# Three shared feed-forward batches in fp32r parts on one Trainium2 core

## The chip, the cores and the metric

One NeuronCore of one Trainium2 chip runs the whole program. The metric is the device time of one execution in microseconds (us), shown as the median of several runs. The profile is one more execution, taken by the hardware profiler, with times from the start of its span. The engines are called as in the profile: PE (TensorE), DVE (VectorE), ACT (ScalarE), POOL (GpSimd) and SP, which only issues transfers here.

## The reference

The kernel computes one transformer layer on `x` (4 batches of 512 rows, 256 wide) and a context of which only the first 512 rows of each batch are seen through the causal mask:

```
x = x + attention(layernorm(x), context)          # 16 heads of 16
h = layernorm(x)                                  # 2048 rows of 256
logits = h @ gate_w.T                             # 8 experts
the two best experts of each row, weights by softmax
out = sum over the two: weight * (silu(h @ wg.T) * (h @ wu.T)) @ w_down.T     # 384 hidden columns
shared = silu(h @ sg_gate.T) * (h @ sg_up.T) @ sg_down.T                      # 384 hidden columns, every row
x = x + shared + out
```

The change lies in the line `shared`, and in the preparation of the expert weights.

## The kernel before

All is float32 in value. A product of two float32 operands runs in one of two ways here. Either both operands are given to PE as float32; or each is split into a high part (an fp32r copy) and a low part (the rest, also fp32r), and PE sums three fp32r products, high x high, high x low and low x high. The experts use the second way, the shared batches the first.

The engines run five programs side by side, ordered by hand, which wait for one another on counted semaphores. After attention the order is this. PE turns the normalised rows `xn2` of a batch into columns `xn2T` (L751), makes the router's logits (L760), and between these the shared feed-forward of a batch `b`: `shared_up` (L854) makes blocks `n = 3b + m`; a block is gate and up for 128 hidden columns and the 512 rows of the batch. ACT takes the silu of the gate half (`shared_silu`, L1145), DVE multiplies it by the up half (`shared_h`, L1397) into `sg`, and `shared_down` (L865) multiplies by `w_sd`; DVE adds the result to the rows (`shared_y`, L1419). Two pairs of PSUM banks hold blocks in turn. Batches 0 to 2 run in this stage, batch 3 at the end of the kernel behind the experts (L999).

DVE's routing runs beside it: the two best experts (L1426 to L1440), the weights, for which ACT makes one exponential (L1158), the ranks by products with triangles of ones (L891), and the slot of each row in lists of 128-row tiles; the lists come from one-hot rows (`hot_slots`, L1492) by 32 products (L906). POOL then gathers rows of a tile by an indirect transfer from the DRAM copy `normed_rows` (`rows_in_tile`, L583). That copy is stored by SP for batches 0 to 2 (L447) and by ACT for batch 3 (L1151).

The expert weights `wup` (two transfers of 3 MB, L454) go out on SP's queue when attention has released its memory. ACT makes the eight high pieces `wup_hi` (`hi_parts`, L1159; 1536 columns each) and DVE the eight low pieces `wup_lo` (`lo_part`, L1498); the first expert product (L933) waits for all eight. From there 39 tiles follow in a loop of fixed order (L975): transposes, three-part products up and down, and an indirect transfer that adds the result rows (L587).

The rows `xn2`, the columns `xn2T` and `sg` lie in one region `moe` (L199). Stores of `xn2` to DRAM must have landed before that part of the region is written again.

## Time and profile before

| | |
|---|---|
| median of 3 runs | 495.11 us (494.94 to 496.69) |
| the profiled execution's own time | 494.46 us |
| its span, first to last instruction | 492.4 us |
| mean granted TensorE clock | 0.995 of full speed |
| busy: PE, DVE, ACT, POOL | 93%, 63%, 43%, 40% of the span |

Matmuls are pipelined, so their durations overlap; the step from one start to the next is what one costs. A float32 product shows as two records. In a row of a timeline stand the start, the duration, the engine, the line, the operation, output and inputs, and the idle time before it with what ended it; "x4" means that four instructions in a row are merged into one.

### The profile page before, as it was taken

The page shows a single profiled execution, that of the slowest core. Times are in us where ns is not written, and L with a number is a line of the kernel's source. Part 1 is how long each engine was busy: PE and PEld are TensorE (multiplying, and loading weights), DVE is VectorE, ACT ScalarE, POOL GpSimd, SP SyncE. Part 2 cuts the span into 40 slices and gives each one's busy share as a digit, 9 for nine tenths or more (in the row PEclk, how much of TensorE's full clock was granted, in tenths as well). Part 3 has the DMA queues.
Part 4 walks back from the last instruction along what each step waited for, and adds up shares of the span by engine and source line. Part 5 has one row for each costly group of instructions (what it writes and reads, how often), then busy time and mean ns, then how long its engine had stood idle before and what let it go on. Part 6 is the DMA issues. An engine that isn't in the chain of part 4 may idle for free.

```text
span 492.4 us, 10465 instructions
## 1 busy us (share of the span) xinstructions
PE 457.4 (93%) x3237; PEld 322.0 (65%) x3238; DVE 312.2 (63%) x651; ACT 211.8 (43%) x421; POOL 196.0 (40%) x204
## 2 busy tenths in 40 slices
PE   7979999999999999999978999999999999999992
PEld 6754444654447444564555546699999999999852
DVE  4985757477563856647975895955455555554446
ACT  2255666527572566656764253332332223223210
POOL 4113544214541337302622003036676666665420
PEclk9999999999999999999999999999999999999997
DMA  8593422422124021310398901014444444444389
GB/s 272 101 230 101 126 72 72 140 69 72 63 76 150 32 97 38 115 64 2 98 379 322 327 2 43 0 39 72 76 64 65 74 75 64 65 72 68 36 208 333
DMA packets 45575, 53.86 MB, mean 109 GB/s; under 512 B 7760, under 2 KB 41872, under 8 KB 44912
## 3 DMA queue, kind: packets, MB, share of 16 engines
q1 hardware_dynamic: 34320, 39.77, 25.2%
q0 software_dynamic: 7488, 10.31, 13.3%
q10 hardware_dynamic: 3744, 3.47, 2.7%
q8 instruction: 14, 0.23, 0.2%
q14 instruction: 9, 0.07, 0.1%
HBM read 27.09 MB, written 13.67 MB: 83 GB/s over the span
## 4 chain that ended last, share of the span: by engine, by line
PE 68%; DVE 15%; ACT 6%; issue 5%; DMA 4%; SPq 1%; POOL 0%; DVEq 0%; ACTq 0%; POOLq 0%
PE set_a L628 7%; PE set_b L658 6%; PE set_a L679 6%; PE set_a L934 6%; PE set_a L933 6%; PE set_a L935 6%; PE set_b L648 4%; DVE attention L1317 3%; ACT attention L1084 3%; PE set_b L952 3%; PE set_a L670 3%; PE set_a L842 3%; PE set_b L953 3%; PE set_b L954 3%; PE set_b L943 2%
## 5 line engine op out<-in xcount | busy, mean ns | idle before, releaser
L1317 DVE TENSOR_REDUCE attention<-set_a 128x2 f32<-128x1024 f32 (+2 forms) x96 | 95.9, 1040 | 25.1 <-PE set_a L630 23.0
L1084 ACT ACTIVATE attention<-set_b 128x512 f32<-128x512 f32 (+1 forms) x176 | 87.8, 570 | 50.2 <-PE set_b L648 36.6
L532 POOL TENSOR_SCALAR_AFFINE_SELECT attention<-attention 128x512 f32<-128x512 f32 x64 | 42.6, 679 | 100.5 <-ACT attention L1084 100.5
L592 POOL DMA_INDIRECT sum_rows<-moe,token_of x39 | 61.8, 1585 | 43.9 <-issue 29.8
L648 PE MATMUL set_b<-attention 99*128 99x512 bf16 (+3 forms) x256 | 59.2, 303 | 7.1 <-ACT attention L1084 5.7
L628 PE MATMUL set_a<-attention 96*128 96x512 bf16 (+3 forms) x256 | 60.5, 302 | 4.9 <-DVE attention L1317 4.7
L1184 ACT ACTIVATE moe<-set_a 128x384 f32<-128x384 f32 x39 | 19.1, 490 | 105.2 <-PE set_a L935 95.6
L584 POOL DMA_INDIRECT e_x<-normed_rows,token_of x39 | 39.4, 1011 | 61.3 <-DVE token_of L1516 34.9
L1541 DVE TENSOR_TENSOR moe<-set_a,moe 128x384 f32<-128x384 f32 x39 | 21.7, 557 | 63.0 <-issue 36.3
L628 PEld LDWEIGHTS set_a<-attention 96*128 96x128 bf16 x256 | 24.9, 97 | 44.3 <-DVE attention L1317 17.2
L933 PE MATMUL set_a<-wup_hi,e_xT_hi 128*128 x156 | 53.0, 340 | 0.0
L934 PE MATMUL set_a<-wup_lo,e_xT_hi 128*128 x156 | 52.8, 339 | 0.0
L935 PE MATMUL set_a<-wup_hi,e_xT_lo 128*128 x156 | 52.8, 338 | 0.0
L630 PE MATMUL set_a<-maskb,identb 128*128 128x128 bf16 x256 | 48.8, 219 | 0.0
L658 PE MATMUL set_b<-attention 128*32 128x128 f32 (+3 forms) x512 | 43.8, 441 | 1.2 <-POOL attention L532 1.1
L952 PE MATMUL set_b<-w_down_hi,e_hT_hi 128*128 x117 | 36.4, 311 | 1.4 <-DVE moe L1553 0.9
L648 PEld LDWEIGHTS set_b<-attention 99*128 99x128 bf16 x256 | 19.1, 97 | 28.4 <-ACT attention L1084 18.8
L513 POOL TENSOR_TENSOR attention<-attention 128x512 f32<-128x512 f32 x14 | 15.9, 1158 | 49.1 <-ACT attention L1005 29.8
L1005 ACT ACTIVATE attention<-set_b 12x512 bf16<-12x512 f32 (+4 forms) x48 | 25.7, 594 | 21.8 <-PE set_b L616 10.9
L1005 ACT ACTIVATE attention<-attention 128x512 bf16<-128x512 f32 x32 | 19.4, 645 | 31.6 <-DVE attention L1265 24.8
L954 PE MATMUL set_b<-w_down_hi,e_hT_lo 128*128 x117 | 32.9, 281 | 0.0
L953 PE MATMUL set_b<-w_down_lo,e_hT_hi 128*128 x117 | 32.8, 281 | 0.0
(169 smaller groups left out, 859.0 us busy)
## 6 DMA issues: line engine op xcount, KB each, us to landing
attention<-attention SPq DMA_DIRECT2D x182, 64.0 KB, 2.6
wup<-in_wupT SPq DMA_DIRECT2D x2, 3072.0 KB, 15.5
sum_rows<-attention SPq DMA_DIRECT2D x2, 2048.0 KB, 13.0
wup<-sum_rows SPq DMA_DIRECT2D x8, 512.0 KB, 7.4
attention<-in_ctxT SPq DMA_DIRECT2D x7, 512.0 KB, 5.6
w_down<-in_wdnT SPq DMA_DIRECT2D x3, 1024.0 KB, 4.9
x_res<-in_x SPq DMA_DIRECT2D x4, 512.0 KB, 6.5
out<-x_res ACTq DMA_DIRECT2D x8, 256.0 KB, 4.0
```

The lines of the kernel that those rows point to most:

```text
L592: g.indirect_dma_start(acc[i], bass.IndirectOffsetOnAxis(token_of[:, t:t + 1], 0), e_y[:, t % 2, :], None, compute_op=ALU.add).then_inc(ad ...
L628: mm(dst, qstack[0:ROWS, g // 2, h, k * P:w], kstack[0:ROWS, g // 2, h, 0:w], start=True, stop=False)
L630: last = mm(dst[:, k * P:w], identb[:], maskb[:], start=False, stop=True)
L648: last = mm(bank(par)[:, i * w:(i + 1) * w], kstack[0:ROWS + 3, g // 2, h, k * P:(k + 1) * P], qstack[0:ROWS + 3, g // 2, h, k * P:S], sta ...
L658: last = mm(pv_bank[32 * h:32 * h + 32, k * P:S], vaug[:, k, HG * g + h, :], pT[k][:, h, :], start=k == 0, stop=k == QT - 1, tile_position ...
L933: mm(dst, e_xT_hi[:, a, c, :], wup_hi[:, c, cols], start=c == 0, stop=False)
L934: mm(dst, e_xT_hi[:, a, c, :], wup_lo[:, c, cols], start=False, stop=False)
L935: last = mm(dst, e_xT_lo[:, a, c, :], wup_hi[:, c, cols], start=False, stop=c == C - 1)
L952: mm(dst, e_hT_hi[:, a, m, :], wdn_hi[:, m, cols], start=m == 0, stop=False)
L954: last = mm(dst, e_hT_lo[:, a, m, :], wdn_hi[:, m, cols], start=False, stop=m == M - 1)
L1084: nc.scalar.activation(pT[k][:, h:h + heads, :], bank(par)[:, 0:heads * (S - k * P)], ACT.Exp).then_inc(b_free, 1)
L1317: v.tensor_reduce(dst, src, AX.X, ALU.max, negate=True).then_inc(a_free, 1)
```

## The change

Gate and up of batches 0 to 2 go over to fp32r parts, all but the first block (`shared_up(0, 0, 1)` stays as it is).

- The parts of `w_sg` and `w_su` lie in `w_parts`, on the rows `xn2` of batches 0 to 2. ACT makes the high ones behind a wait for these rows' three stores, POOL the low ones.
- ACT makes the high part of a batch's columns (`rows_hi`). That of batch 0 has a buffer of its own; those of batches 1 and 2 share the place of batch 3's rows, and in front of the first of them ACT waits for all four stores (`act.wait_ge(xn_stored, DMA * B)`), ahead of the second silu and of the exponential. DVE makes the low parts of batches 0 and 2 (`rows_low`), POOL that of batch 1.
- `shared_up_parts` takes the place of `shared_up`: per block and half, and per half of the 256 inputs, three products of 512 columns.
- The expert weights' two transfers count on two semaphores. ACT makes the high pieces one at a time between the silus; POOL makes the low pieces of the first four and of the last of them, DVE the other three.
- PE's order changes: blocks 1 and 2 before the ranks, block 3 behind them, and the products of the lists behind the second down group. DVE's one-hot rows and the second batch's multiplications are moved with it.

```diff
@@ -132,7 +132,11 @@
             pass
+        with nc.sbuf_tensor("moe_parts", [P, MOE], F32R) as moe_r:
+            pass
         moe = sb("moe", [P, MOE])
+        with nc.sbuf_tensor("first_rows_hi", [P, C, S], F32R) as first_hi:
+            pass
         e_xT_hi = sb("e_xT_hi", [P, 2, C, P], F32R)
@@ -201,6 +205,11 @@
         lgT = sg[:, M - 1, :]
+        w_parts = moe_r[:, 0:4 * C * HALF].rearrange("p (i a c n) -> p i a c n", i=2, a=2, c=C)
+        later_hi = moe_r[:, (B - 1) * QT * D:B * QT * D].rearrange("p (c n) -> p c n", c=C)
+        x_hi = [first_hi[:], later_hi, later_hi]
+        xT_parts = moe_r[:, T * D:T * D + C * N].rearrange("p (c n) -> p c n", c=C)
+        x_lo = [xT_parts[:, :, b * S:(b + 1) * S] for b in range(B - 1)]
         TE = T * E
...
@@ -451,7 +464,7 @@
             for c in range(C):
-                sp.dma_start(wup[:, c, :], wupT[c * P:(c + 1) * P]).then_inc(ld_up, DMA)
+                sp.dma_start(wup[:, c, :], wupT[c * P:(c + 1) * P]).then_inc(ld_up[c], DMA)
             sp.wait_ge(who_ready, TOP_K)
@@ -549,6 +562,9 @@
+            for a, w in enumerate((wsg, wsu)):
+                pool.wait_ge(sw_hi, a + 1)
+                g.tensor_tensor(w_parts[:, 1, a], w[:], w_parts[:, 0, a], ALU.subtract).then_inc(sw_lo, 1)
             pool.wait_ge(a_free, A_ALL)
@@ -574,6 +590,17 @@
+            pool.wait_ge(sx_hi, 2)
+            pool.wait_ge(s_up, 1)
+            g.tensor_tensor(x_lo[1], xn2T[:, :, S:2 * S], x_hi[1], ALU.subtract).then_inc(sx_lo[1], 1)
+
+            def up_low(i):
+                pool.wait_ge(up_hi, i + 1)
+                w = PIECES[i]
+                g.tensor_tensor(piece(wup_lo, w), piece(wup, w), piece(wup_hi, w), ALU.subtract).then_inc(up_lo, 1)
+
+            for i in range(EARLY):
+                up_low(i)
             pool.wait_ge(pad_rows, DMA)
@@ -594,6 +621,7 @@
                 rows_in_tile(t)
+            up_low(SPLITS - 1)
             for t in range(NX, NX + 2):
@@ -862,6 +890,21 @@
+            def shared_up_parts(b, lo=0, hi=M):
+                pe.wait_ge(sw_lo, 2)
+                pe.wait_ge(sx_lo[b], 1)
+                for m in range(lo, hi):
+                    n = b * M + m
+                    if n > 1:
+                        pe.wait_ge(s_h, n - 1)
+                    for a, dst in enumerate(gu[n % 2]):
+                        for c in range(C):
+                            high, low = (w_parts[:, i, a, c, m * P:(m + 1) * P] for i in range(2))
+                            mm(dst, high, x_hi[b][:, c, :], start=c == 0, stop=False)
+                            mm(dst, high, x_lo[b][:, c, :], start=False, stop=False)
+                            last = mm(dst, low, x_hi[b][:, c, :], start=False, stop=c == C - 1)
+                    last.then_inc(s_up, 1)
+
             def shared_down(b):
@@ -886,7 +929,7 @@
             pe.wait_ge(lg_read, 1)
-            shared_up(0, 1, 2)
+            shared_up_parts(0, 1)
@@ -897,10 +940,11 @@
             last.then_inc(rank_full, 1)
-            shared_up(0, 2)
+            shared_up_parts(1, 0, 1)
             pe.wait_ge(rank_read, 2)
             shared_down(0)
-            shared_up(1)
+            shared_up_parts(1, 1)
+            shared_down(1)
@@ -908,8 +952,7 @@
             last.then_inc(hot_full, 1)
-            shared_down(1)
-            shared_up(2, 0, 2)
+            shared_up_parts(2, 0, 2)
@@ -957,7 +1000,7 @@
             rows_t(0, 0, 0, 1, True)
-            shared_up(2, 2, 3)
+            shared_up_parts(2, 2)
             rows_t(1, 1, 1, 1)
@@ -1137,8 +1180,16 @@
+            def rows_hi(b):
+                copy(x_hi[b], xn2T[:, :, b * S:(b + 1) * S]).then_inc(sx_hi, 1)
+
             ln2_copies(2)
+            act.wait_ge(xn_stored, DMA * (B - 1))
+            act.wait_ge(ld_moe, DMA * 4)
+            for a, w in enumerate((wsg, wsu)):
+                copy(w_parts[:, 0, a], w[:]).then_inc(sw_hi, 1)
             logits_copy(0, slice(0, S - P), pv_bank[:, 0:S - P])
+            rows_hi(0)
             deviations(3, T - QT, T)
@@ -1154,25 +1205,36 @@
+            act.wait_ge(xn_stored, DMA * B)
+            rows_hi(1)
+            shared_silu(0, 1)
             act.wait_ge(d_ready, 1)
             nc.scalar.activation(ex, dl, ACT.Exp).then_inc(ex_ready, 1)
-            def hi_parts(pieces):
-                for i in pieces:
-                    copy(piece(wup_hi, i), piece(wup, i)).then_inc(up_hi, 1)
-
-            for m in range(1, M):
-                shared_silu(0, m)
-            act.wait_ge(ld_up, DMA * C)
-            hi_parts(range(0, EARLY))
-            for m in range(M):
-                shared_silu(1, m)
+            shared_silu(0, 2)
+
+            def hi_part(i):
+                copy(piece(wup_hi, PIECES[i]), piece(wup, PIECES[i])).then_inc(up_hi, 1)
+
+            act.wait_ge(ld_up[0], DMA)
+            hi_part(0)
+            hi_part(1)
+            act.wait_ge(s_y, 1)
+            shared_silu(1, 0)
+            hi_part(2)
+            shared_silu(1, 1)
+            hi_part(3)
+            shared_silu(1, 2)
+            rows_hi(2)
+            act.wait_ge(ld_up[1], DMA)
+            act.wait_ge(hot_full, 1)
+            hi_part(EARLY)
+            hi_part(EARLY + 1)
+            shared_silu(2, 0)
             act.wait_ge(lists_ready, 1)
             act.wait_ge(who_stored, DMA)
-            hi_parts(range(EARLY, EARLY + 1))
-            shared_silu(2, 0)
-            hi_parts(range(EARLY + 1, EARLY + 2))
+            hi_part(EARLY + 2)
             shared_silu(2, 1)
-            hi_parts(range(EARLY + 2, SPLITS))
+            hi_part(EARLY + 3)
@@ -1399,7 +1461,12 @@
+            def rows_low(b):
+                dve.wait_ge(sx_hi, b + 1)
+                v.tensor_tensor(x_lo[b], xn2T[:, :, b * S:(b + 1) * S], x_hi[b], ALU.subtract).then_inc(sx_lo[b], 1)
+
             shared_h(0, 0)
+            rows_low(0)
             steps = [0]
@@ -1438,6 +1505,7 @@
                 v.tensor_copy(who[:, :, TOP_K + k:TOP_K + k + 1], i_k.rearrange("p (t o) -> p t o", o=1))
+            shared_h(0, 1)
             dve.wait_ge(ex_ready, 1)
@@ -1469,15 +1537,13 @@
                 link(v.tensor_reduce(slotf[:, k, :], oh, AX.X, ALU.add))
-            shared_h(0, 1)
+            shared_h(0, 2)
...
             v.tensor_scalar(own_lo, slot_lo, -1.0, io_p, ALU.mult, ALU.add)
-
-            shared_h(0, 2)
@@ -1497,17 +1563,18 @@
                 dve.wait_ge(up_hi, i + 1)
-                v.tensor_tensor(piece(wup_lo, i), piece(wup, i), piece(wup_hi, i), ALU.subtract).then_inc(up_lo, 1)
-
-            hot_slots(range(0, T))
+                w = PIECES[i]
+                v.tensor_tensor(piece(wup_lo, w), piece(wup, w), piece(wup_hi, w), ALU.subtract).then_inc(up_lo, 1)
+
+            shared_h(1, 0)
+            hot_slots(range(0, T // 2))
             shared_y(0)
+            hot_slots(range(T // 2, T))
+            shared_h(1, 1)
             hot_slots(range(T, T + T // 2))
-            shared_h(1, 0)
+            shared_h(1, 2)
             hot_slots(range(T + T // 2, NJ)).then_inc(hot_built, 1)
-            shared_h(1, 1)
-            lo_part(0)
-            shared_h(1, 2)
-            lo_part(1)
+            rows_low(2)
@@ -1515,11 +1582,9 @@
             shared_y(1)
-
-            lo_part(2)
             shared_h(2, 0)
-            lo_part(3)
             lo_part(EARLY)
+            lo_part(EARLY + 1)
             shared_h(2, 1)
@@ -1557,12 +1622,10 @@
-            lo_part(EARLY + 1)
             rows_lo(0, 0)
...
             rows_lo(1, 1)
-            lo_part(EARLY + 3)
             weights(0, 0, True)
```

`PIECES` is `[0, 1, 2, 3, 6, 7, 4, 5]`, the order in which the pieces are made.

## Rows read from the trace of the kernel before

**Rows 1.** The page, first part: busy time of each engine.

```profile
PE 457.4 (93%) x3237; PEld 322.0 (65%) x3238; DVE 312.2 (63%) x651; ACT 211.8 (43%) x421; POOL 196.0 (40%) x204
```

**Rows 2.** Stages: length, each engine's busy us, clock, DMA share, GB/s.

```profile
274.60:318.60 44.00, 42.87 (x197) 26.48 (x197) 37.09 (x84) 17.84 (x20) 4.91 (x5) 1.00 0.22 68
318.60:462.00 143.40, 142.94 (x978) 140.15 (x977) 76.87 (x223) 43.02 (x112) 90.52 (x71) 1.00 0.41 65
```

**Rows 3.** Chain of waits, shared stage: start, us, engine, output, line.

```profile
295.80 1.18 PE set_b L908 x32
296.98 5.26 PE set_b L871 x24
...
302.23 6.88 PE set_a L861 x16
```

**Rows 4.** Timeline of PE: the first expert tile's products.

```profile
318.59 0.53 PE L933 MATMUL set_a<-wup_hi,e_xT_hi 128*128 x1
...
319.31 0.34 PE L933 MATMUL set_a<-wup_hi,e_xT_hi 128*128 x1
...
320.72 0.34 PE L935 MATMUL set_a<-wup_hi,e_xT_lo 128*128 x1
```

**Rows 5.** Lines 449 and 1151: the stores of the normalised rows.

```profile
L449 SPq DMA_DIRECT2D normed_rows<-moe x3: 359/1354/2333, 251.4 to 256.8; - x3
...
DMA to landing us min/median/max: 6.9/8.0/8.8
...
L1151 ACTq DMA_DIRECT2D normed_rows<-moe x1: 409/409/409, 267.1 to 267.1; - x1
...
DMA to landing us min/median/max: 17.4/17.4/17.4
```

**Rows 6.** DMA queues, 274 to 275 and 280 to 281 us: packets, MB, share.

```profile
q1 hardware_dynamic: 17, 0.42, 96.9%
q10 hardware_dynamic: 17, 0.02, 4.9%
...
q10 hardware_dynamic: 281, 0.29, 80.7%
```

**Rows 7.** Timeline of ACT between the last LayerNorm and the expert weights.

```profile
265.19 0.20 ACT L1010 ACTIVATE std<-st_a 128x4 f32<-128x4 f32 x1 [1.82 <-DVE st_a L1245]
...
274.42 0.22 ACT L1158 ACTIVATE router<-router 128x16 f32<-128x16 f32 x1 [3.22 <-DVE router L1437]
274.65 1.28 ACT L1147 ACT_TABLE_LOAD   x1
275.94 0.60 ACT L1147 ACTIVATE moe<-set_a 128x512 f32<-128x512 f32 x1
...
282.89 5.61 ACT L1005 ACTIVATE wup_hi<-wup 128x1536 fp32r<-128x1536 f32 x4 [2.96 <-DMA wup<-in_wupT]
```

**Rows 8.** Timeline of DVE: the ranks' read and the last one-hot rows.

```profile
275.80 0.17 DVE L1449 COPY router<-set_b 128x8 f32<-128x8 f32 x1 [0.44 <-PE set_b L898]
...
291.96 1.38 DVE L1495 TENSOR_SCALAR router<-router 128x128 bf16<-128x128 bf16 x8
```

**Rows 9.** Lines 501, 1339 and 1242: ns shortest, median, longest; first, last start.

```profile
L501 POOL TENSOR_TENSOR x_res<-x_res,attention x4: 2368/2372/3336, 70.6 to 242.4; 128x1024 f32 x3, 128x1024 f32<-128x1024 f32 x1
...
L1339 DVE TENSOR_TENSOR w_down_lo<-w_down,w_down_hi x6: 1212/1648/3393, 236.4 to 243.4; 128x1024 fp32r<-128x1024 f32 x6
...
L1242 DVE TENSOR_SCALAR st_c<-st_c x4: 162/214/606, 6.2 to 264.6; 128x4 f32<-128x4 f32 x2, 128x12 f32<-128x12 f32 x2
```

**Rows 10.** Timeline of POOL: the first gather.

```profile
300.18 1.15 POOL L584 DMA_INDIRECT e_x<-normed_rows,token_of  x1 [34.88 <-DVE token_of L1516]
```

**Rows 11.** Stages at the end of the span, columns as in rows 2.

```profile
483.50:484.00 0.50, 0.21 (x1) 0.00 (x0) 0.29 (x2) 0.00 (x0) 0.00 (x0) 1.00 1.10 350
487.00:487.50 0.50, 0.00 (x0) 0.00 (x0) 0.50 (x2) 0.00 (x0) 0.00 (x0) 0.66 1.10 387
```

**Rows 12.** Timeline of PE: the first products of the run.

```profile
3.28 6.58 PE L687 MATMUL set_b<-beforeb,identb 128*128 128x128 bf16 x64 [3.28 <-POOL beforeb L484]
```

More of the change, by code:

```diff
@@ L245, in build @@
         ld_x = [sem(f"ld_x{b}") for b in range(B)]
-        ld_k, ld_q, ld_ctx, ld_v, ld_o, ld_cv, ld_moe, ld_up = (sem(n) for n in
-            ("ld_k", "ld_q", "ld_ctx", "ld_v", "ld_o", "ld_cv", "ld_moe", "ld_up"))
+        ld_k, ld_q, ld_ctx, ld_v, ld_o, ld_cv, ld_moe = (sem(n) for n in
+            ("ld_k", "ld_q", "ld_ctx", "ld_v", "ld_o", "ld_cv", "ld_moe"))
+        ld_up = [sem(f"ld_up{c}") for c in range(C)]
         consts, pads, fills, pad_rows = sem("consts"), sem("pads"), sem("fills"), sem("pad_rows")
@@ L272, in build @@
         s_up, s_sg, s_h, s_y, s_yfree = (sem(n) for n in ("s_up", "s_sg", "s_h", "s_y", "s_yfree"))
+        sw_hi, sw_lo, sx_hi = sem("sw_hi"), sem("sw_lo"), sem("sx_hi")
+        sx_lo = [sem(f"sx_lo{b}") for b in range(B - 1)]
         e_in = [sem(f"e_in{i}") for i in range(NX)]
@@ L351, in build @@
         EARLY = 4
+        PIECES = [0, 1, 2, 3, 6, 7, 4, 5]
         def piece(w, i):
```

## The prediction, made before the changed kernel was timed

> **What bounds the kernel now.** Read the page first: PE is busy for 93% of the span, POOL for 40% [rows 1]. Then cut the span into stages: between 274.6 and 318.6 us, where the three shared batches run, PE is busy 42.87 of 44.00 us, and in the expert tiles up to 462 us 142.94 of 143.40 [rows 2]. So PE sets the pace on both sides of the edit. The chain of waits says the same with the lines: in this stage it runs from one group of products to the next, two shared blocks (gate and up of 128 hidden columns, 16 records) in 6.88 us, 3.44 each, a down group in 5.26, the one-hot products in 1.18 [rows 3]. The first expert product starts at 318.59 [rows 4]. What stands behind it follows as it did, so I work out when that product starts in the changed kernel and move the end by as much. The profiled execution took 494.46 us (span 492.4), 0.65 below the median of 495.11; the sum is made against 494.46 and 0.65 is added at its end.
>
> **What the products save.** An fp32r product of 384 columns follows the one before it every 0.176 us: eight steps from 319.31 to 320.72 [rows 4]. In proportion, 512 columns take 0.235. A block becomes 2 x 2 x 3 = 12 such products, 2.82 us against 3.44, 0.62 less. The fastest end would be 0.176 again, 2.1 us a block; slower than in proportion I leave out, since the form is the same. Eight blocks change (the first one stays as it is): 4.9 us less on PE, and up to 10.6 at that end.
>
> **What the parts need, and where that is late.** I follow ScalarE, whose queue is in order. (1) The weights' parts lie on the stored rows of batches 0 to 2, so ScalarE waits for three stores. The last is issued at 256.8 and the three land in 6.9 to 8.8 us [rows 5]: 263.7 at the earliest. Two copies of 768 follow (four of 1536 take 5.61 us [rows 7], so 0.70 each), then the logits copy and the high part of batch 0, 0.94. The square root of the last LayerNorm, at 265.19 before [rows 7], comes some 1.4 us later, and its normalising on DVE may wait for POOL's two weight subtractions too: the router starts 1.4 to 3 us late. That costs nothing as long as the next wait ends later still, and it does.
>
> (2) Before the second silu stands a wait for all four stores, since the high parts of batches 1 and 2 lie on batch 3's rows. The fourth goes out on ScalarE's queue at 267.1 and lands 17.4 us later, at 284.5 [rows 5]. The reason shows in the packets: from 274 to 275 us the queue of the expert weights moves 17 packets and this queue 17, but the weights' are 24 KB and fill 96.9% of the 16 engines, the store's are 1 KB [rows 6]. From 280 to 281 us, with the weights nearly done, the store moves 281 packets of its 512 [rows 6]. Nobody waited for it before: the gather that reads it starts at 300.18 [rows 10]. In the changed kernel the weights are issued as before and the store a little later, so it still ends behind them. The router's 2048 small writes, which shared its last 2 us, come later than it now; I take 283.2 as the landing, with 281.8 (0.8 us behind that burst) and 284.5 as ends.
>
> (3) Behind that wait stand the high part of batch 1 (0.94 to 1.0), the second silu (0.60), a table load (1.28) and the router's exponential (0.22) [rows 7]: ready at 286.3, where it was at 274.64. Everything on DVE from there on (ranks, lists) hangs on it, 11.7 us late. PE gets its two blocks of batch 0 and the ranks done by about 280.4 and stands (the ranks ended at 275.8 before [rows 8]; up to 3 us for the late router, some 1.6 for the part of the second block that the selection doesn't cover). Its next block needs POOL's low part of batch 1: 1024 columns, 2.37 us undisturbed [rows 9], so 283.2 + 1.0 + 2.4 + 0.1 = 286.7.
>
> **What follows, by PE alone.** From 286.7 on PE still has six blocks (16.9), three down groups (15.8), the one-hot products (1.2) and two pairs of transposes (0.4): 34.3 us, first expert product at 321.0, 2.4 us later than before. The hole of 6 us has a price of its own. At the end of the run the granted clock was 1.00 (2.4 GHz) while PE worked, up to 483.71, and 0.50 (1.2 GHz) from about 487.2, after 3.5 us of nothing [rows 11]; I expect the same in the hole. What the return takes shows at the start of the run, where 64 products of 128 columns take 6.58 us [rows 12], 103 ns each; 128 columns are 107 ns at 1.2 GHz and 53 at 2.4, so most of these 6.6 us passed at the low level. I take 4.5 us of it here, 2.2 us lost (ends 0 and 3.3). Then 323.3, later by 4.7.
>
> **By DVE's chain.** From the exponential at 274.64 to the end of the one-hot rows at 293.25 [rows 8], DVE took 18.6 us. The changed order keeps these instructions and adds a product of 0.6: built at 286.3 + 18.6 + 0.6 - 0.4 (the wait for the ranks [rows 8], which are long there) = 305.1. Behind them come 1.2 + three blocks 8.5 + 0.4 + the last down group 5.3 = 15.4 us on PE: 320.5. Undisturbed, this chain is just behind PE's.
>
> It isn't undisturbed. POOL now makes four low parts in the same stretch (the fifth comes in the gathers' shadow), each 1536 columns, 2.37 x 1.5 = 3.55 us. POOL's one long subtraction of before that met DVE's at 242.4 took 3.34 us instead of 2.37, and DVE's beside it 3.39 us, where the shortest of that line took 1.21: it stood until POOL was through [rows 9]. Single-input forms stand too: a scalar form of 12 columns took 0.61 us beside POOL's masks, where the shortest of that line took 0.16 [rows 9]. The Trainium skill, page "SBUF — State Buffer", section "Who interferes with whom", has this as an exclusive lock of a port pair for a whole instruction, which DVE forms with two SBUF inputs take against POOL's reads, and its copies and scalar forms in a two-port mode too; both rows agree with it, and by it the term below would come out at its upper end, which speaks against this part of the change. The ends: 0, if each part falls into a wait of DVE, and 4 x 3.55 = 14.2, if each stands in front of DVE in full. I take half, 7.1: the first two parts (from about 289.6) meet two-input fp32 instructions of the ranks, which the rows show standing; the last two meet the one-hot rows, bf16 and one input, for which no row of before decides. So: built at 312.2, first expert product at 327.6, 9.0 us later than before.
>
> **Other edits.** The five low parts leave DVE, but behind the lists, where DVE waits for PE anyway: nothing. Loading the expert weights on two semaphores lets ScalarE begin after the first half; but ScalarE stands until 283.2, when both halves are there (the first high part of before waited for them until 282.89 [rows 7]): nothing. The one-hot products now stand behind the second down group, and only two blocks (5.6 us) cover lists, gather issue and landing. Lists take 0.5 on DVE, and the gather's issue 1.15 [rows 10], which leaves 3.9 for its landing; that time is not shown (the stores took 6.9 and more, in full queues [rows 5]). I take 0, with 3 us as the far end. The last high part on ScalarE and its low part on POOL end some 2 us before the first expert product: 0.
>
> **Forecast.** 494.46 + 9.0 + 0.65 = 504.1, say 504 us, slower by 1.8%.
>
> **Rivals.** (a) *The hole isn't there*: the fourth store lands before PE has run out of work (280.4). Then 4.9 us are saved, the router's delay gives back 1.4 to 3, and PE's own short waits may close: 494.46 - 4.9 + 2 + 0.65 = 492, with 489 as the lower end. For it: the store is small, 512 KB. Against: it had 17.4 us in the profile with the same weights in flight and is now issued later. 0.08. (b) *A short hole*: it lands at 281.8, the clock doesn't fall, POOL's parts fall into DVE's waits: 321.0 - 1.4, so 496.1; with the landing at 283.2, 497.5. It decides if DVE is at its waits for PE each time a high part is ready. 0.15, and just over half of that lies within 0.5%. (c) *The one-hot rows stand too*: POOL's other two parts stand in front of DVE as well, the lists are built at 319.3 and the first expert product starts at 334.7: 511 us. In rows: the single-input form of 0.61 us [rows 9] is for it, that those were fp32 and not bf16 against. 0.14. This is what the rule of the Trainium skill named above ("SBUF — State Buffer", "Who interferes with whom") gives, if the one-hot rows run in a two-port mode; no row here shows which mode they are in. (d) *Something beyond*: the shared stage within 0.5% for reasons I don't see, 0.03.
>
> **Numbers.** The main case, 500 to 508, has 0.60. Half a per cent, 2.5 us, is about what a measurement of this kernel can tell from no change. Slower by more than that: 0.60 + 0.14 + 0.07 of (b) = 0.81. Within: 0.08 of (b) and (d), 0.11. Faster: 0.08. The range from 496.5 to 511.5 takes in the main case, most of (b) and (c), and leaves out (a), and the edges of the others, about 0.2.
>
> **What would show it.** In the changed profile: ScalarE idle from about 272 to 283, released by the store on its own queue (or by nothing named); the exponential at about 286; an empty slice in PE's line near 281 to 286 with a granted clock below 1.00 behind it; POOL's subtractions at 3.5 us or more with DVE instructions of some 3 us beside them; the first expert product near 327 and the expert tiles unchanged behind it. I am wrong if the exponential comes before 280 (the store was early), if PE's blocks take other than about 2.8 us at the full clock, or if the low parts cross DVE without long instructions.

## The result, and the profile after

The changed kernel takes 516.92 us (514.79 to 519.99, 6 runs) against 495.64 (494.91 to 499.74, 6 runs) for the kernel before, measured together: a ratio of 1.0422 [1.0381, 1.0463], slower by 21.3 us. The prediction was slower, 504.0 us, with a range of 496.5 to 511.5. The sign was right and the size less than half of what it is. The profiled execution took 519.99, with a span of 517.9.

First part of the page, changed kernel: PE is busy for 8.3 us more and for a smaller share than in [rows 1], though its products take less time at the full clock; POOL has 24.3 us more.

```profile
PE 465.7 (90%) x3269; PEld 336.8 (65%) x3270; DVE 325.9 (63%) x648; ACT 216.4 (42%) x426; POOL 220.3 (43%) x212
```

**Where the 25.5 us of span are.** I cut at two instructions that both kernels have: ScalarE's (ACT's) last standard deviations of 12 columns ahead of the edit (249.45 before, 254.81 after), and the first expert product (318.59 [rows 4], and 344.10). Stages of the kernel before, columns as in rows 2 (the engines in the order PE, PEld, which is PE's loading of weights, DVE, ACT, POOL):

```profile
249.45:318.59 69.14, 63.74 (x364) 40.56 (x357) 52.96 (x133) 28.47 (x39) 7.43 (x16) 1.00 0.49 173
```

Stages of the changed kernel, the whole stage, five stretches in it, and the expert tiles:

```profile
254.81:344.10 89.29, 68.05 (x397) 53.07 (x389) 66.88 (x131) 32.70 (x44) 32.71 (x24) 0.87 0.38 135
281.00:289.50 8.50, 8.50 (x56) 6.83 (x56) 3.71 (x15) 0.00 (x0) 0.00 (x0) 0.76 0.59 215
289.50:293.10 3.60, 0.10 (x4) 0.00 (x1) 1.10 (x2) 3.48 (x5) 2.34 (x1) 0.83 0.00 0
293.10:298.40 5.30, 5.24 (x12) 4.18 (x13) 4.93 (x12) 4.18 (x4) 2.40 (x1) 0.50 0.17 6
314.00:319.00 5.00, 0.00 (x0) 0.00 (x0) 5.00 (x8) 1.51 (x2) 2.93 (x1) 1.00 0.00 0
319.60:323.00 3.40, 3.40 (x10) 2.64 (x10) 3.40 (x17) 0.00 (x0) 0.00 (x0) 0.55 0.00 0
344.10:487.50 143.40, 143.15 (x977) 140.09 (x977) 76.37 (x223) 43.02 (x112) 89.79 (x70) 1.00 0.41 65
```

The stage grew from 69.14 to 89.29, by 20.15. The expert tiles are what they were in [rows 2]: PE busy for 143.15 of 143.40. The other 5.36 lie ahead of the edit and belong to that execution (the last experiment but two). So from here on I compare the length of this stage. A time marked "aligned" is one of the changed kernel less 5.36, to be read against the prediction's.

Inside the stage PE runs at 0.76 of the clock for 8.5 us, is empty for 3.6, then runs at half the clock for 5.3; later it is empty again while DVE is busy for all of the 5 us, and again at about half the clock behind it. The timeline of PE in the changed kernel, the products before which it waited longest, and what released them (327.28 and 332.61 are the first and the 24th product of two blocks):

```profile
276.00 1.97 PE L785 MATMUL set_b<-ident,moe 128*128 128x128 f32 x8 [3.86 <-DVE moe L1315]
...
293.16 0.77 PE L903 MATMUL set_a<-moe_parts 128*128 128x512 f32 x1 [3.56 <-POOL moe_parts L595]
...
304.83 3.10 PE L914 MATMUL set_b<-w_sd,moe 128*128 128x256 f32 x8 [2.64 <-DVE moe L1462]
...
319.14 7.13 PE L914 MATMUL set_b<-w_sd,moe 128*128 128x256 f32 x24 [5.21 <-DVE x_res L1489]
...
327.28 0.47 PE L903 MATMUL set_a<-moe_parts 128*128 128x512 f32 x1
...
332.61 0.39 PE L905 MATMUL set_a<-moe_parts 128*128 128x512 f32 x1
...
341.54 1.99 PE L914 MATMUL set_b<-w_sd,moe 128*128 128x256 f32 x8 [1.63 <-DVE moe L1462]
...
344.10 0.44 PE L976 MATMUL set_a<-wup_hi,e_xT_hi 128*128 x1 [0.56 <-issue]
```

The wait of 3.56 is the hole of the prediction; that of 3.86 ahead of it is the late router. The three on DVE's lines behind the hole (2.64, 5.21 and 1.63) are longer in sum (9.5 us). The timeline of ACT in the changed kernel shows the hole's cause, the fourth store's wait, and behind it the exponential, which stands at 274.42 in [rows 7]:

```profile
289.57 1.06 ACT L1048 ACTIVATE moe_parts<-moe 128x1024 fp32r<-128x1024 f32 x1 [9.50 <-DMA normed_rows<-moe]
...
292.43 0.22 ACT L1212 ACTIVATE router<-router 128x16 f32<-128x16 f32 x1
```

Then the two timelines that explain the rest, to be laid beside each other. POOL's subtractions in the changed kernel:

```profile
290.71 2.34 POOL L595 TENSOR_TENSOR moe_parts<-moe,moe_parts 128x1024 fp32r<-128x1024 f32 x1 [14.73 <-ACT moe_parts L1048]
296.00 6.85 POOL L600 TENSOR_TENSOR wup_lo<-wup,wup_hi 128x1536 fp32r<-128x1536 f32 x2 [2.94 <-ACT wup_hi L1048]
310.02 6.91 POOL L600 TENSOR_TENSOR wup_lo<-wup,wup_hi 128x1536 fp32r<-128x1536 f32 x2 [7.17 <-ACT wup_hi L1048]
...
335.82 3.44 POOL L600 TENSOR_TENSOR wup_lo<-wup,wup_hi 128x1536 fp32r<-128x1536 f32 x1
```

DVE in the same stretches:

```profile
291.15 0.69 DVE L1462 TENSOR_TENSOR moe<-set_a,moe 128x512 f32<-128x512 f32 x1 [6.07 <-ACT moe L1198]
...
296.42 3.08 DVE L1535 TENSOR_SCALAR expert_f<-router 128x39 f32<-128x39 f32 x1
299.54 3.35 DVE L1536 CAST expert_of<-expert_f 128x39 int32<-128x39 f32 x1
...
310.11 7.85 DVE L1561 TENSOR_SCALAR router<-router 128x128 bf16<-128x128 bf16 x8
317.87 1.21 DVE L1489 TENSOR_TENSOR x_res<-set_b,x_res 128x1024 f32<-128x1024 f32 x1
...
322.80 1.38 DVE L1561 TENSOR_SCALAR router<-router 128x128 bf16<-128x128 bf16 x8
...
335.81 5.07 DVE L1567 TENSOR_TENSOR wup_lo<-wup,wup_hi 128x1536 fp32r<-128x1536 f32 x1
```

A cast of 39 columns takes 3.35 us, and eight one-hot rows take 7.85 where another eight take 1.38 a little later. One by one the records show that each of POOL's first four subtractions of 1536 columns held one DVE instruction: the scalar form and the cast end within 0.05 us of POOL's first two, the first two one-hot rows take 3.48 and 3.46 and end within 0.05 us of the next two, and the other six take 0.24 each. Not every form stood: the multiplication at 291.15, one of whose inputs is in PSUM, took its usual 0.69 inside POOL's 2.34 from 290.71. While an instruction is held, DVE is "busy" in the profile's sense, so no wait is shown on it; the wait appears one engine on, on PE. Such a busy number is read as work only if the same line has the same duration elsewhere.

### The profile page after: what moved, and what is told of

Same layout as the page of the kernel before. It is cut to its first block, busy times and chain, and to the rows that moved or that the text cites. A ratio compares the mean times of both kernels' runs of the same rounds, so it can differ in the third digit from the quotient of the medians.

```text
span 517.9 us, 10548 instructions
## 1 busy us (share of the span) xinstructions
PE 465.7 (90%) x3269; PEld 336.8 (65%) x3270; DVE 325.9 (63%) x648; ACT 216.4 (42%) x426; POOL 220.3 (43%) x212
## 3 DMA queue, kind: packets, MB, share of 16 engines
q0 software_dynamic: 7488, 10.31, 12.5%
## 4 chain that ended last, share of the span: by engine, by line
PE 60%; DVE 20%; DMA 8%; ACT 6%; issue 5%; SPq 1%; DVEq 0%; ACTq 0%; POOLq 0%
PE set_a L656 7%; PE set_b L686 6%; PE set_a L976 5%; PE set_a L977 5%; PE set_a L978 5%; PE set_a L707 4%; PE set_b L676 4%; DVE attention L1379 3%; ACT attention L1127 3%; PE set_b L995 3%; PE set_a L870 3%; DMA normed_rows<-moe 3%; PE set_b L996 2%; PE set_b L997 2%; PE set_b L986 2%
## 5 line engine op out<-in xcount | busy, mean ns | idle before, releaser
L656 PE MATMUL set_a<-attention 96*128 96x512 bf16 (+3 forms) x256 | 62.2, 308 | 5.0 <-DVE attention L1379 4.8
L656 PEld LDWEIGHTS set_a<-attention 96*128 96x128 bf16 x256 | 25.5, 100 | 45.0 <-DVE attention L1379 17.4
L611 POOL DMA_INDIRECT e_x<-normed_rows,token_of x39 | 40.5, 1037 | 30.5 <-DVE token_of L1583 12.0
L658 PE MATMUL set_a<-maskb,identb 128*128 128x128 bf16 x256 | 50.1, 224 | 0.0
L914 PE MATMUL set_b<-w_sd,moe 128*128 128x256 f32 x96 | 25.0, 418 | 9.5 <-DVE x_res L1489 5.2
## 6 DMA issues: line engine op xcount, KB each, us to landing
sum_rows<-attention SPq DMA_DIRECT2D x2, 2048.0 KB, 12.7
```

What stands on the lines that cost most here:

```text
L656: mm(dst, qstack[0:ROWS, g // 2, h, k * P:w], kstack[0:ROWS, g // 2, h, 0:w], start=True, stop=False)
L658: last = mm(dst[:, k * P:w], identb[:], maskb[:], start=False, stop=True)
```

## The experiments

Runs of the kernel before stood beside each group: 494.89 (7 runs) beside the first four, 495.99 (19) beside the next four, 495.87 (21) beside the last two.

| kernel | median, us | ratio to before | stage, us |
|---|---|---|---|
| before | 495.64 | | 69.14 |
| changed | 516.92 | 1.0422 [1.0381, 1.0463] | 89.29 |
| before + store wait | 505.44 | 1.0189 [1.0142, 1.0236] | 78.31 |
| before + low parts on POOL | 511.20 | 1.0319 [1.0269, 1.0370] | 84.43 |
| changed, no store wait | 510.97 | 1.0279 [1.0215, 1.0344] | 85.06 |
| changed, low parts on DVE | 504.22 | 1.0172 [1.0131, 1.0213] | 77.39 |
| changed, neither | 500.77 | 1.0117 [1.0060, 1.0175] | 72.01 |
| and router on time | 495.30 | 0.9979 [0.9949, 1.0010] | 67.97 |
| and POOL without subtractions | 494.65 | 0.9976 [0.9944, 1.0007] | 68.06 |
| and DVE reordered | 494.08 | 0.9960 [0.9928, 0.9992] | 65.77 |
| and low products last | 491.09 | 0.9909 [0.9879, 0.9940] | see there |

The stage is that of the one profiled execution, from the standard deviations to the first expert product.

**The store wait alone.** In the kernel before, ahead of the exponential:

```diff
+            act.wait_ge(xn_stored, DMA * B)
             act.wait_ge(d_ready, 1)
```

> The kernel before, with nothing added but the wait for all four stores ahead of the router's exponential and the second silu. Theory (the hole and the standing of DVE behind POOL add up): the exponential moves from 274.6 to about 284.7 us, PE stands from 279 to about 290 (the first down group waits for the second silu, which DVE takes up only behind the ranks), the granted clock falls in that hole, and the end moves by 11 to 13 us: 506 to 508. Rival, POOL's low parts alone make the loss: PE catches up and it stays within 2 us of 495.

Measured 505.44, 0.6 below the expected range; the stage is 9.17 longer. The timeline of ACT in this kernel:

```profile
286.47 0.21 ACT L1159 ACTIVATE router<-router 128x16 f32<-128x16 f32 x1 [8.35 <-DMA normed_rows<-moe]
```

Alone, by the stage, the wait is worth what the prediction gave to the whole change (9.0). The store that nobody waited for before is indeed late, and the exponential with it.

**POOL's low parts alone.** In the kernel before, POOL makes the first four low parts, DVE's four calls go:

```diff
+            for i in range(EARLY):
+                pool.wait_ge(up_hi, i + 1)
+                g.tensor_tensor(piece(wup_lo, i), piece(wup, i), piece(wup_hi, i), ALU.subtract).then_inc(up_lo, 1)
...
-            lo_part(0)
...
```

> The kernel before, with nothing changed but that POOL makes the first four low parts of the up weights in place of DVE. Theory: each of POOL's 3.5 us subtractions stands in front of one DVE instruction of the lists or the one-hot rows for up to 3.3 us; between 284 and 292 us two of them meet the lists (7 us of DVE), the other two come later; DVE saves 7 us of its own low parts behind the lists, but the lists are on the path: 3 to 7 us slower, 498 to 502. Rival, the two engines don't stand behind each other and only the hole costs: 494 to 496, or a little faster.

Measured 511.20: far above it. The stage is 15.29 longer. POOL's timeline in this kernel, and DVE's beside it:

```profile
285.91 15.81 POOL L579 TENSOR_TENSOR wup_lo<-wup,wup_hi 128x1536 fp32r<-128x1536 f32 x4 [18.59 <-ACT wup_hi L1008]
```

```profile
285.61 1.46 DVE L1491 TENSOR_TENSOR router<-router 128x1248 bf16<-128x1248 bf16 x1
286.99 4.71 DVE L1492 TENSOR_TENSOR router<-router 128x1248 bf16<-128x1248 bf16 x1
291.62 12.27 DVE L1498 TENSOR_SCALAR router<-router 128x128 bf16<-128x128 bf16 x16
...
304.94 1.38 DVE L1498 TENSOR_SCALAR router<-router 128x128 bf16<-128x128 bf16 x8
```

PE stood for the multiplication behind these rows, and its next products took 3.78 us where such four take 1.9 at the full clock:

```profile
306.97 3.78 PE L864 MATMUL set_a<-moe,w_sg 128*128 128x512 f32 x4 [13.31 <-DVE moe L1403]
```

DVE's second and third row take 16.98 us; undisturbed they take 1.46 (the row above, of the same shape) and twice 1.38, 4.2 in sum. So 12.8 us of DVE went for 15.8 us of POOL, and the four subtractions taken from DVE were worth 4 x 1.75, behind the lists. The one-hot rows, bf16 and with one input, stand like the others: the question that the prediction left open ("for which no row of before decides") is answered, and its rival (c) has its mechanism. The Trainium skill, page "SBUF — State Buffer", section "Who interferes with whom", gives the same: the loser of the port pair is blocked in full, copies and scalar forms in a two-port mode among them. That the one-hot rows stood, the 12.27 us show; in which mode they run, no row shows.

**The change without the store wait.** Batch 1's high part gets a buffer of its own, and the wait goes behind the silus of batch 1:

```diff
-        x_hi = [first_hi[:], later_hi, later_hi]
+        x_hi = [first_hi[:], second_hi[:], later_hi]
...
-            act.wait_ge(xn_stored, DMA * B)
             rows_hi(1)
...
+            act.wait_ge(xn_stored, DMA * B)
             rows_hi(2)
```

> The changed kernel, with the high part of batch 1 in memory of its own (that of the gathered rows, which come later), so that the wait for all four stores stands only ahead of batch 2's. Theory: the exponential moves from 287 to about 282 (it then waits for the first block in parts, which runs at the low clock), 5.5 us, and one loss of the clock of some 2 us goes: 6 to 8 us faster than the changed kernel, 507 to 510; POOL's parts still stand in front of DVE. Rival, the hole is the whole loss: 494 to 498. Rival, POOL's parts are the whole loss: no change, 514 to 517.

Measured 510.97, 1 above the expected range and outside both rivals'. The stage loses 4.23 of its 20.15. In this kernel too eight one-hot rows take 7.83 us.

**The change with the low parts on DVE.** `up_low` goes from POOL, `lo_part` takes its pieces, two of them behind the one-hot rows but ahead of the last step of the lists (DVE's sum of what PE made of these rows):

```diff
-            for i in range(EARLY):
-                up_low(i)
...
             rows_low(2)
+            lo_part(0)
+            lo_part(1)
...
```

> The changed kernel, with all eight low parts of the up weights on DVE again, behind the lists as before; the wait for the stores stays. Theory: the 13 us that DVE stood (3.1 + 3.4 in front of the experts' numbers, 6.5 in the one-hot rows) and 3 more at the end of the stage go, and the hole of 5 us with a loss of the clock is left: 499 to 502. Rival, the hole is the whole loss: no change, 514 to 517. Rival, POOL's parts are the whole loss: 492 to 496.

Measured 504.22, 2 above the expected range. The stage loses 11.90, with the store wait still there. The timeline of DVE in this kernel, same instructions as above:

```profile
295.64 0.19 DVE L1532 TENSOR_SCALAR expert_f<-router 128x39 f32<-128x39 f32 x1
295.86 0.18 DVE L1533 CAST expert_of<-expert_f 128x39 int32<-128x39 f32 x1
...
304.55 1.39 DVE L1558 TENSOR_SCALAR router<-router 128x128 bf16<-128x128 bf16 x8
```

Against the changed kernel: 3.08 - 0.19, 3.35 - 0.18 and 7.85 - 1.39 are 12.5 us, in front of the lists, for 13.8 us of POOL.

**Neither.** Both edits together.

> The change with the wait for the fourth store taken away (the high part of batch 1 has a buffer of its own, so nothing is overwritten) and with all low parts of the up weights on VectorE. Theory (the hole of PE, POOL's low parts standing in front of VectorE, and the clock lost behind both make up the loss): against the change without the wait (510.97) the low parts are worth some 12, as they were with the wait in (516.92 to 504.22); so 497 to 501 us. What is left is the late router (some 3 us) against 4.9 us saved on products. The exponential comes some 3 to 4 us later than in the kernel before, and the stage from the standard deviations to the first expert product takes 70 to 73 us. Rival (the two losses are one and the same time, and each experiment took away most of it): 503 to 505, as with the low parts alone. Second rival (the products save what was predicted and nothing else is left): 490 to 492.

Measured 500.77 (497.01 to 502.69, 5 runs), in the theory's range and below the first rival's; its profiled execution is the shortest of the five. The exponential came 30.76 us behind the standard deviations, where it comes after 24.97 in the kernel before: 5.8 later, not 3 to 4. With the four kernels a square is closed: the low parts on POOL are worth 11.9 of the stage with the store wait and 13.1 without it, the store wait 4.2 with the low parts on POOL and 5.4 without, and 2.9 are left with neither. By the medians it is 12.7 and 10.2, 6.0 and 3.5, and 4.8, with about 1 us between the groups in the kernel before itself. In the changed kernel the two losses add up, to within 1.2 us by the stage and 2.5 by the medians; they aren't the same time. Alone, in the order of the kernel before, they are 9.17 and 15.29, which need not add up to the changed kernel's.

**The router on time.** What is left has its own cause:

```diff
             ln2_copies(2)
+            logits_copy(0, slice(0, S - P), pv_bank[:, 0:S - P])
             act.wait_ge(xn_stored, DMA * (B - 1))
...
-            logits_copy(0, slice(0, S - P), pv_bank[:, 0:S - P])
-            rows_hi(0)
             deviations(3, T - QT, T)
```

`rows_hi(0)` comes back in front of the last logits copy, and the low parts of `w_sg` and `w_su` go from POOL to DVE, behind `shared_h(0, 0)`.

> The kernel without the wait and with the low parts on VectorE, and in it the work that stood ahead of the router moved behind what the router needs: on ScalarE the logits copy goes ahead of the two weight copies and the high part of batch 0 goes behind the last deviations; the weights' low parts go from POOL to VectorE, behind the first shared product. Theory: the router starts within 1 us of the kernel before, and the stage shrinks by 2 to 4 us against the kernel without that edit: 493 to 498 us, near or just under the kernel before. Rival (the router's start is covered by PE's first block, as the prediction had it): no change, 497 to 501.

Measured 495.30 (10 runs): 5.5 less by the medians, 4.0 by the stage. This edit also takes two subtractions from POOL, so the 4 us belong to both together. With the store wait gone, the work ahead of the router does cost; in the change itself it seems to lie under the wait (see the changed kernel once more).

**POOL without subtractions.** `x_lo[1]` on DVE as well, ahead of `shared_h(0, 1)`:

```diff
-            g.tensor_tensor(x_lo[1], xn2T[:, :, S:2 * S], x_hi[1], ALU.subtract).then_inc(sx_lo[1], 1)
...
+            rows_low(1)
             shared_h(0, 1)
```

> As the kernel with the router on time, and the low part of batch 1 also on VectorE, so POOL makes no subtraction in this stage. Theory: POOL's one remaining part costs VectorE about what it takes on POOL (2.4 to 3.3 us), VectorE makes it in some 1.3, so VectorE gains 1 to 2 us; PE is the bound by then, so 0 to 2 us less than the kernel before it: 491 to 498. Rival (VectorE is now the bound because it carries all): 1 to 2 us more.

Measured 494.65: 0.65 less than the kernel before it, with intervals that overlap, so nothing is decided between the two theories. But the stage shows why the saved products are not seen in the end. Stages of this kernel, columns as in rows 2:

```profile
251.42:319.48 68.06, 59.65 (x397) 47.57 (x389) 57.76 (x138) 32.65 (x44) 9.63 (x17) 0.97 0.50 176
```

PE is busy for 59.65 instead of 63.74, 4.1 less, near the 4.9 of the prediction. DVE is busy for 57.76 instead of 52.96, 4.8 more: two subtractions of weights (0.95 each) and three of rows (1.22 each) make 5.6. Timeline of PE in this kernel, where the 4 us went:

```profile
307.14 0.41 PE L955 MATMUL set_b<-ident,e_x 128*128 128x128 f32 x2 [1.47 <-DMA e_x<-normed_rows,token_of]
...
312.56 0.66 PE L955 MATMUL set_b<-ident,e_x 128*128 128x128 f32 x2 [2.25 <-DVE e_xT_lo L1592]
313.02 6.81 PE L906 MATMUL set_b<-w_sd,moe 128*128 128x256 f32 x24
```

DVE in the same stretch:

```profile
299.25 3.41 DVE L1563 TENSOR_TENSOR wup_lo<-wup,wup_hi 128x1536 fp32r<-128x1536 f32 x2
302.58 0.22 DVE L1579 TENSOR_REDUCE router<-set_b 128x39 f32<-128x78 f32 x1
...
306.40 5.09 DVE L1563 TENSOR_TENSOR wup_lo<-wup,wup_hi 128x1536 fp32r<-128x1536 f32 x3
```

Two low parts stand in front of the lists' last step (302.58), so the gather is late; three stand in front of the first tile's rows. And the down group that follows takes 6.81 instead of 5.26 [rows 3].

**The change once more**, for the stretch ahead of the edit.

> The changed kernel once more, for the stretch ahead of the edit. In its first profile the last standard deviations before the router came at 254.81 us, in the kernel before at 249.45, with the same instructions ahead of them; the four other changed kernels had 251.4 to 254.4. If the 5.4 us belong to the execution, this profile shows another value in 249 to 255 and the stage behind it takes again about 89 us; if they belong to the change, it shows 254 to 255 again.

One execution, 515.16. The standard deviations came at 250.23 and the first expert product at 339.76: 89.53, where the first profile had 89.29. So the 5.36 us belong to the execution. The rest came again: PE's hole was 4.45, the three waits on DVE's lines 2.79, 5.19 and 1.63, the cast 3.35 and the eight one-hot rows 7.85. The last standard deviations ahead of the router were only 1.5 us late, where the first profile has 3.0, and the exponential came no sooner for it (37.96 behind the standard deviations of 12 columns, against 37.62). Over the twelve profiles that instruction of 12 columns came between 249.45 and 254.81, and the mean granted clock from 44 to 52 us was 1.00 in the eight earliest of them and 0.79 in the four latest; what decides it wasn't tried.

**DVE reordered.** From the kernel in which POOL makes no subtraction:

```diff
             rows_low(2)
-            lo_part(0)
-            lo_part(1)
+            shared_y(1)
...
-            shared_y(1)
-            lo_part(2)
+            lo_part(0)
+            lo_part(1)
             shared_h(2, 0)
...
+            lo_part(2)
             rows_lo(0, 0)
-            lo_part(EARLY + 2)
+            shared_h(2, 1)
+            lo_part(3)
             shared_h(2, 2)
             rows_lo(1, 1)
-            lo_part(EARLY + 3)
+            for i in range(EARLY, SPLITS):
+                lo_part(i)
```

The last high part goes behind the first tile's rows on ACT.

> The kernel in which POOL makes no subtraction, with VectorE's work behind the one-hot rows in another order: the lists and the second residual sum come ahead of the first two low parts, each of the first two expert tiles' low rows ahead of low parts that nobody waits for yet, and on ScalarE the last high part goes behind the first tile's rows. No work is added or taken away. In the kernel with the old order PE waited 1.47 us for the first gather and 2.25 for the first tile's low rows, and VectorE was busy without a break from the ranks to the last low part. Theory (VectorE now sets the time of the first expert product, because the parts of the shared rows and weights moved about 5 us of work to it while PE got 4 us shorter): the two waits go, but the wait for the last low part takes their place; 0 to 2.5 us less, 492 to 494.7. Rival (the two waits alone set the end): 3.7 us and the clock's loss behind them come back, 489 to 491.

Measured 494.08 (11 runs), ratio 0.9960 [0.9928, 0.9992]: the theory's range. The stage is 65.77, 2.3 shorter than without this edit and 3.4 shorter than in the kernel before; by the medians the edit is worth 0.6. Timeline of PE in this kernel:

```profile
316.97 0.43 PE L968 MATMUL set_a<-wup_hi,e_xT_hi 128*128 x1 [3.11 <-DVE wup_lo L1563]
```

Both earlier waits are gone, and the wait for the last low part is in their place. DVE waited for another engine twice between 269 us and that point, 0.6 us in all.

**The low products last.** So the first expert tile does first what needs no low part:

```diff
-            pe.wait_ge(up_lo, SPLITS)
+            pe.wait_ge(up_hi, SPLITS)
             pe.wait_ge(s_h, (B - 1) * M)
-            up(0, 0, first[0])
+            up_low_last(0, 0, first[0])
```

In `up_low_last` the eight products with `wup_hi` come first, then the wait for `up_lo`, then the four with `wup_lo`.

> As the kernel with VectorE reordered, and the first expert tile takes its eight products with the high parts of the weights first and its four with the low parts last, so PE has some 1.4 us of work while VectorE makes the last low part. Theory (VectorE's last low part is what PE waits for): 1 to 2 us less than the kernel without that edit, 490.5 to 493.5. Rival (PE is not waiting there): no difference.

Measured 491.09 (489.88 to 494.44, 11 runs), ratio 0.9909 [0.9879, 0.9940]: 0.9% faster than the kernel before, clear of the noise, and inside the expected range. Its interval overlaps a little with that of the kernel without this edit, so the 3 us between these two are a rough figure. Timeline of PE:

```profile
318.26 0.94 PE L971 MATMUL set_a<-wup_lo,e_xT_hi 128*128 x4 [1.68 <-DVE wup_lo L1579]
```

The wait is 1.68 instead of 3.11: shorter by 1.43, which is what the eight products take (8 x 0.18). PE still waits there for DVE. The two profiled executions differ by 0.2 only (492.20 and 491.99): in this one the exponential came 28.16 us behind the standard deviations, against 26.84 without the edit, 1.3 later ahead of all that the edit touches. The 3 us between the medians are not all explained by the 1.4.

## Why the prediction was wrong in size

*What bounds the kernel, and where the change acts*: right. Behind the first expert product nothing changed, and the stage's growth is the loss.

*The products*: right. Two blocks at the full clock start at 327.28, and their 24th product at 332.61: 0.232 a step, 2.78 a block, predicted 0.235 and 2.82.

*The late stores, the wait, the exponential*: right in place and nearly in time. The third store let ACT go at 268.71 (aligned 263.35, predicted 263.7); the fourth at 289.57 (284.2; 283.2); the exponential was ready at 292.65 (287.3; 286.3). The weight subtractions of POOL delayed the last standard deviations by 3.0 us and the turning of these rows on PE by 3.6, past the 1.4 to 3 of the prediction (1.5 and 2.5 in the second execution). The exponential was no later in the execution with the later router, which fits the prediction's "costs nothing as long as the next wait ends later"; whether the fourth store, which goes out behind it, would have landed sooner wasn't tried.

*The hole and its clock*: right in kind, too long in size. It is 3.56 us and not 6 (4.45 in the second execution), because PE came to it later, having waited 3.9 us in the late router (for the normalised rows) and run the blocks behind that at a low clock (0.76 from 281 to 289.5 us). Behind it the clock was 0.50 and a block took 5.2 us (from 293.16 to 298.4) instead of 2.78: 2.4 lost, predicted 2.2.

*The step that failed* is the one that says "I take half, 7.1". Its first half was right: two parts stood in front of the ranks' instructions. The second was not: the last two stood in front of the one-hot rows, 6.5 us, so that 12.5 of the 13.8 us lay in front of the lists. They were built at 324.18 (aligned 318.8) instead of 312.2: 6.6 later, of which the standing behind POOL is 5.4 and the exponential 1.0. The value to take was near the upper end, 14.2, which the text had from the row of 0.61 us and from the page of the Trainium skill that it names, and put down to a rival with 0.14.

*A second term was too small*: the way from the lists to the first expert product, predicted at 15.4 us and 19.9 long. PE came to the one-hot products only at 326.11, 1.9 behind the lists: its second down group, which the new order puts ahead of the one-hot products, had waited 5.2 us for `shared_y(0)`, which stood on DVE behind the eight one-hot rows that POOL held, and then ran in part at 0.55 of the clock (7.13 us instead of 5.26). For this order the prediction reckoned with the gather's landing alone (0, at most 3 us). The sentence on the fifth low part, "in the gathers' shadow", fell too: at 335.82 it stood in front of DVE's own low part (5.07 instead of 1.75), the last `shared_h` came late, and the last down group waited 1.63 for it. With the 9.0 that was predicted, 6.6 and 4.5 make 20.1, the whole growth of the stage. The prediction followed DVE's standing to the lists and no further; what is late on DVE is also late for whoever waits for it.

*Rivals.* (c), 511 us by the one-hot rows, had the mechanism; 6 us of it were missing. (a) with 492 if the hole isn't there was too hopeful: with neither the store's wait nor POOL's low parts the kernel still takes 500.77, in part because of the work ahead of the router (4.0 us by the stage, 5.5 by the medians), in part because DVE gets what PE is spared. That last point was not in the prediction; the order of DVE's work and of the first expert products was worth 3.6 us by the medians (494.65 to 491.09) once the rest was mended.

## What to carry to other kernels

An elementwise instruction on POOL is not free because POOL is idle. Where DVE has work at the same time, price it as time of DVE: here 0.8 to 0.9 us of DVE for each us of POOL's subtractions, with DVE's forms of one input and in bf16 among those that stood, and the multiplication with an input in PSUM not among them. Then follow what is queued behind them. When products go from PE to parts made by DVE, add up DVE's stage as well as PE's: here 4.1 us left one and 4.8 came to the other, and the gain appeared only when DVE's late results were asked for in the order in which they come.

## What the runs showed that I had not expected

- DVE's cast of 39 columns took 3.35 us beside POOL's subtraction and 0.18 without, and eight bf16 one-hot rows 7.85 and 1.39: small one-input instructions are held as long as large ones. Of the eight rows two were held, one by each subtraction.
- POOL seems to stand too. Of its four subtractions back to back (15.81 us) the first two took 4.46 and 4.64, beside DVE's 1248-column instructions with two inputs, and the last two 3.41 each, beside the one-hot rows; in the changed kernel a pair takes 6.85. The first began at 285.91, while DVE's 1.46 us from 285.61 were still running.
- Ahead of the edit, executions differ by up to 5.4 us with the same instructions, beside a granted clock of 0.79 or 1.00 between 44 and 52 us.
